# Identity turns on TensorE behind the first maxima of an attention kernel

## The reference

```python
qkv = (tokens @ w_proj + b_proj).reshape(B, N, 8, 48)       # 8 heads of 16
attn = softmax(einsum('bihd,bjhd->bijh', q, k) * 16 ** -0.5, axis=2)
out = einsum('bijh,bjhd->bihd', attn, v) @ w_out + b_out + tokens
t = out + spike_attn(layernorm(out))     # thresholds on q, k, v; causal mask of score > 0.1
t = t + moe(layernorm(t))                # 8 experts, 128 -> 512 -> 128, GELU, the best expert of each token
```

## Time and profile before

| | |
|---|---|
| time, median of 3 runs | 1120.28 us (1116.77 to 1126.87) |
| profiled execution, its own time | 1123.22 us |
| its span, first to last instruction | 1121.5 us |
| TensorE, VectorE, ScalarE, GpSimd busy | 1064.6, 880.7, 787.3, 323.7 us |
| mean granted TensorE clock | 0.957 |

### The profile page before, as it was taken

One profiled execution on the slowest core, in us unless ns is written; L12 is line 12 of the kernel. 1 busy time (PEld: TensorE's weight loads), 2 busy tenths in 40 slices (PEclk: granted clock), 3 DMA queues, 4 the chain that ended last, 5 costly groups with the idle time before them and its releaser, 6 DMA issues. The chain is left out here.

```text
span 1121.5 us, 23624 instructions
## 1 busy us (share of the span) xinstructions
PE 1064.6 (95%) x7976; PEld 482.0 (43%) x7984; DVE 880.7 (79%) x1975; ACT 787.3 (70%) x1693; POOL 323.7 (29%) x384
## 2 busy tenths in 40 slices
PE   5999999999999999999999999999899997899994
PEld 2122323333232333323323333332366776899993
DVE  4999989988988988898899899994177785654446
ACT  2277877877878877888878788788666644655553
POOL 4041031113105103210410410006324565675550
PEclk7599999999999999999999999999999896999996
DMA  4417004303500710440260053000060112223318
GB/s 123 94 42 164 4 1 132 77 8 80 130 2 12 178 20 1 114 96 1 58 152 2 1 147 43 2 2 20 10 179 18 37 34 71 70 78 83 86 39 302
DMA packets 58635, 76.09 MB, mean 68 GB/s; under 512 B 15464, under 2 KB 33896, under 8 KB 58520
## 3 DMA queue, kind: packets, MB, share of 16 engines
q1 hardware_dynamic: 53368, 63.67, 23.6%
q0 software_dynamic: 4320, 8.89, 2.4%
q10 hardware_dynamic: 832, 2.03, 0.5%
HBM read 47.64 MB, written 26.65 MB: 66 GB/s over the span
## 5 line engine op out<-in xcount | busy, mean ns | idle before, releaser
L738 DVE TENSOR_REDUCE neg_half<-slot 128x1 f32<-128x512 f32 x1024 | 643.8, 682 | 73.1 <-PE slot L519 67.9
L651 ACT ACTIVATE probs<-ring 128x512 f32<-128x512 f32 x1024 | 542.0, 600 | 140.0 <-PE ring L528 139.7
L528 PE MATMUL ring<-stack_q,stack_k 50*128 50x512 bf16 (+1 forms) x2048 | 418.1, 381 | 1.3 <-issue 1.3
L519 PE MATMUL slot<-stack_k,stack_q 48*128 48x512 bf16 x1024 | 378.9, 391 | 14.6 <-DMA stack_q<-parts_dram 10.1
L562 PE MATMUL acc<-probs,v_sb 128*32 128x512 f32 x2048 | 272.8, 605 | 0.0
L528 PEld LDWEIGHTS ring<-stack_q,stack_k 50*128 50x128 bf16 (+1 forms) x2048 | 117.7, 94 | 270.9 <-issue 232.4
L519 PEld LDWEIGHTS slot<-stack_k,stack_q 48*128 48x128 bf16 x1024 | 96.0, 94 | 147.5 <-DVE neg_half L738 84.8
L1666 ACT ACTIVATE mask<-bank,w_of 128x128 f32<-128x128 f32 x284 | 81.1, 369 | 55.9 <-PE bank L1632 55.9
L437 POOL CAST m_parts<-neg_max 128x16 bf16<-128x16 f32 x32 | 6.3, 198 | 327.6 <-DVE neg_max L744 327.6
L1605 POOL DMA_INDIRECT rows_tok<-mask,x_in x71 | 68.9, 970 | 57.0 <-DVE mask L1700 52.1
L1632 PE MATMUL bank<-xt,w_of 128*128 128x128 f32 x568 | 78.0, 281 | 5.2 <-DVE w_of L1690 3.3
(11 more groups left out here) (168 smaller groups left out, 1017.9 us busy)
## 6 DMA issues: line engine op xcount, KB each, us to landing
parts_dram<-parts SPq DMA_DIRECT2D x30, 384.0 KB, 4.9
stack_k<-parts_dram SPq DMA_DIRECT2D x32, 192.0 KB, 3.9
stack_q<-parts_dram SPq DMA_DIRECT2D x64, 96.0 KB, 3.8
x_in<-rows_in SPq DMA_DIRECT2D x71, 64.5 KB, 2.2
xp<-in_x SPq DMA_DIRECT2D x8, 512.0 KB, 5.0
stack_k<-parts_dram SPq DMA_DIRECT2D x32, 128.0 KB, 3.5
xr<-in_x SPq DMA_DIRECT2D x8, 512.0 KB, 3.7
out<-zt SPq DMA_DIRECT2D x16, 256.0 KB, 2.1
```

The costliest lines, as they stand in the source:

```text
L519: return pe.matmul(out[:, :], queries(u, BB, q % 2, ht)[rows, qt * P:(qt + 1) * P], stack_k[u % STACK_BUFS][rows, BB, ht, half * HALF:(hal ...
L528: return pe.matmul(out[:, :], stack_k[s % STACK_BUFS][rows, run, ht, kt * P:(kt + 1) * P], queries(s, run, half, ht)[rows, :], start=run = ...
L651: act.activation(probs[:, j % PROBS, h, :], ring[n % S_BANKS][:, :], ACT.Exp).then_inc(s_empty[n % S_BANKS], 1)
L738: dve.tensor_reduce(neg_half[q % 2][:, half, k:k + 1], slot[n % M_BANKS][:, :], AX.X, ALU.max, negate=True).then_inc(m_empty[n % M_BANKS], 1)
```

## The change

A constant `SOLO_TURNS = 8` is added. The loop of twelve turns becomes a function `keep_on(turns)`, called with 12 in its old place, and with 8 behind each solo job whose first tile is below 22, which are the eleven solos ahead of the first front. The turns wait for no semaphore and add to none. They write the four quarters of `acc`, two times each.

```diff
+SOLO_TURNS = 8
...
+            def keep_on(turns):
+
+                for n in range(turns):
+                    pe.transpose(acc[:, n % 4 * P:(n % 4 + 1) * P], ident[:, :], ident[:, :])
+
             pe.wait_ge(s_const, 1)
-            for n in range(12):
-                pe.transpose(acc[:, n % 4 * P:(n % 4 + 1) * P], ident[:, :], ident[:, :])
+            keep_on(12)
             for job in ORDER:
                 kind, args = job
                 if kind in ("stats", "aggr"):
                     continue
                 if kind in ("front", "rear", "solo"):
                     rounds(job)
+                    if kind == "solo" and args[0] < AHEAD_FIRST:
+                        keep_on(SOLO_TURNS)
                     continue
```

## The result

The changed kernel takes 1142.86 us in the median of 4 runs (1138.47 to 1145.64), the kernel before 1122.76 in the 4 beside it. The ratio is 1.0169, 95% interval 1.013 to 1.0208: 15 to 23 us slower. The two medians alone are 20.1 us apart. Forecast were 1133.8 us, in a range that ends at 1138; that stood on a median before of 1120.28, of 3 runs. The spans of the two profiled executions, 1121.5 and 1136.6, are 15.1 apart, where 13.5 were forecast. Measured again, the ratio was 1.0153 (1.0126 to 1.018). All ratios are of fast runs, without one of 5500.82 us with four turns and two of 1139.95 and 1140.17 us in the run with 80 turns ahead and eight behind each solo.

A forecast was written before the change was run, and what follows sets the result against it. VectorE was taken to bound the solos, TensorE the stretch from the first score. Eleven solos add 14.2 us, give-back returns 0.7: +13.5 on the median of 1120.28 gives 1133.8 us, range 1121 to 1138.

The forecast's parts named there:

- What bounds the kernel, and what is covered: Opening: VectorE bounds the solos, TensorE from the first score; eight turns, 1.75 us, exceed the low-clock cover of 0.73.
- The cover of 0.73 us: Behind a solo's last maximum at 1.2 GHz: VectorE's three reductions hide turns for 1.80 - 0.64 - 0.43 = 0.73 us.
- The price of a cycle: Each of eleven solos at 1.2 GHz: 3.65 us on TensorE against 2.40 before, 1.25 more.
- The turns' rate: Turns behind the solos at 1.2 GHz: 0.218 us each, taken from the twelve turns at the start.
- The other row of the prediction: Turns at the kernel's end, at low clock: 0.236 us each, 1.89 for eight; used for the upper bound of +15.8.
- +14.2: First score, after eleven solos of 3.65 us: at 61.1 us instead of 46.96, so 14.2 us later.
- The give-back: Stretch from the first score on: an earlier clock rise returns 0.7 us, within bounds of nothing and 2.5.
- No rise among the solos: Eleven solos of the opening: clock stays at 0.50 despite the turns, net +13.5 us; chance 0.64.
- (a): Rival, eleven solos: the clock rises within them and stays; +2.2 us after three solos, 1120 to 1129 us; chance 0.30.
- (b): Rival, solos: turns beside row-tiled work cost under 0.09 us each and stay under the cover; 1120.3 us; chance 0.04.
- Rival (a)'s sum for the full clock: Solos at 2.4 GHz: eight turns take 0.91 us, fit a cover of 1.16 and cost nothing; rival's chance 0.30.

The follow-up runs named there:

- the run with two: Two turns behind each of the eleven solos instead of the changed kernel's eight; ratio 1.0026 (0.9995 to 1.0056) to the kernel before.
- two sixes: Changed kernel with twelve turns per solo, six behind the third and six behind the fourth maximum; ratio to before 1.0031, with 80 turns ahead 1.0017.

## Why the prediction was wrong

The direction and the mechanism were right, the size wasn't. By its own steps:

**What bounds the kernel, and what is covered.** Right that VectorE bounds the solos before and TensorE after, and that an us lost ahead of the first score is lost at the end of the attention (17.1 us there, 16.5 at the first score). The cover of 0.73 us was mis-sized; measured is 0.29. It took VectorE to hold three whole reductions when the last maximum begins. But when that maximum begins (26.50), the first of the three has already run for 0.15 us, so 1.65 us are left and not 1.80; then come 0.64 of latency, 0.54 instead of 0.43 to the first turn, and 0.18 for a block: 1.65 - 0.64 - 0.54 - 0.18 = 0.29. Since eight turns are far beyond either, this had no part in the forecast's miss.

**The price of a cycle** is the step that failed. 1.47 + 0.43 + 1.75 = 3.65 was forecast, and 1.39 + 0.53 + 1.90 = 3.82 measured, 0.17 more for each of eleven. The wait for the bank was a little shorter. The turns' rate was right (0.215 in a block against 0.218). What was missing are the 0.18 us by which a block between maxima is longer than its turns' streams, and the 0.1 to change over to it. The other row of the prediction, 1.89 us for eight turns, which was taken for the bound alone, had the size of the whole block (1.90). The eleven cycles make 1.9 us. Another 0.22 is the turn of the maxima itself, which now stands between two solos (55.78 to 56.00) and which the sum left out. So +14.2 became +16.5.

**The give-back** of 0.7 us was 0 in the first profile and 2.4 in the second; both are within the bounds of 0 and 2.5, whose upper end was measured at 2.8 (7.32 to 4.51) where the clock was up all the time. In the profiles it goes with how early the clock rises.

**No rise among the solos** was right for the change as made, in both profiles, and 42.4 us in both. The reason wasn't a general one: sixteen turns lift it. As to the Trainium skill's statement in "TensorE: Matmul & The Clock Gate", Part 4, that transposes don't bring the full clock on, the trace with sixteen turns disagrees as the earlier trace rows did.

**What wasn't in the sum** is what comes behind 90 us. The wait for the maxima's rows came out 0.5 us longer than in the first profile of before, which by the second one is chance. The fall of the clock behind it cost 1.5 more; it is in both profiles of the changed kernel and in neither of before, and whether it is the change's stays open. Thus 16.5 us are shown as the change's own. The intervals allow 15 to 23 and 14 to 20 us.

The measured time is 9.1 us above the forecast. Of these, 2.5 are the median of before, which a fourth run took from 1120.28 to 1122.76, and 2.3 are the price of the solos. The remaining 4.3 are the give-back of 0.7, which didn't come in the first profile, what comes behind 90 us, and scatter; the runs don't divide them further. The range's upper end had only 1.6 us of price, the 0.7 of give-back and 2 us of scatter above the forecast, and no term for the stages behind the change.

The rivals: (a), a rise among the solos, didn't happen with eight turns; (b), turns under the cover, is excluded by the run with two. Rival (a)'s sum for the full clock was about right: eight turns in one piece took 1.03 us at 2.4 GHz (25.56 less 24.53 in the run with 80 ahead) instead of 0.91. That is 0.11 past the cover for each solo and not under it, and the clock didn't stay up in that run.

## What to carry to other kernels

Filler work for a clock must be priced at the clock at which it begins: at 1.2 GHz it costs nearly twice (eight turns 1.90 us against 1.03), and if it doesn't lift the clock, that is all that it does. The form that cost nothing measurable here was one long unbroken piece where the engine waits anyway (the 10 us ahead of the first stacks, to 0.5 us ahead of the first maximum), and then small pieces laid into each wait for a bank, not behind the whole group. Even that form won no time that could be told from none. For a block put between other matmuls add its change-over, here 0.28 us at 1.2 GHz, and check the cover in the steady cycle, not for one group with all buffers full.

## What the runs showed of the hardware that was not expected

- The same eight turns per solo, at full clock: in one piece, the clock fell after three solos in the profile; in two pieces, with 90 turns ahead instead of 80 and a pause of 0.48 us instead of 1.57, it stayed up in the profile, and the mean clock of all twelve runs was high.
- Full-height fp32 turns among maxima of 48 rows lifted the clock from 0.50 with sixteen in one piece and with two sixes, not with eight in one piece or in two.
- At 1.2 GHz a block of fp32 turns between bf16 maxima takes 0.18 us more than its turns at 0.215 us each, and the maxima ahead hold it up by 0.1 us.
- TensorE's full clock on the same work of the lead was worth 2.8 us of 7.3, less than half of it. VectorE was then busy for 4.33 of 4.40 us, ScalarE for 3.56.
- Of 14 loads that SyncE's queue issues one behind the other in some 0.60 us each, one took 0.96 to 2.24 us in ten of the fourteen profiles, at different places of the row, and the DMAs behind it in the queue were issued later.
